# Two-step opening of the last batch sums, two bias rows moved later, and an early Gelu table load, in a four-layer transformer kernel

## Chip, cores and metric

The kernel runs on one core of one Trainium2 chip. The metric is the device time of one execution in microseconds (us); the lower, the better. Times of instructions below are from the profiled execution, counted from the start of its span.

## The reference

Eight batches of 128 tokens with 512 channels (float32) go through four layers. Each layer adds an attention and then a feed-forward to x, each of the layernorm of x. Cut to what matters here:

```python
x = x + L0_xattn(layernorm(x), ctx, ...)   # 32 heads of 128, own keys and values per head
x = x + L0_ffn(layernorm(x), ...)          # silu, 1376 hidden, low-rank parts
x = x + L1_xattn(layernorm(x), ctx, ...)   # small attention of 8 heads of 8
x = x + L1_ffn(layernorm(x), ...)          # 1792 hidden, one of each 32 picked
x = x + L2_xattn(layernorm(x), ctx, ...)   # 32 heads, 8 key heads, normed q and k
x = x + L2_ffn(layernorm(x), ...)          # mixture of low-rank experts
x = x + L3_xattn(layernorm(x), ctx, ...)   # 32 heads, 8 key heads, biases bq, bkv, bo
x = x + L3_ffn(layernorm(x), ...)          # gelu(x @ inter_w + inter_b) @ output_w + output_b
```

The row `L3_bo` is the output bias of layer 3's attention and the row `F3_bias` that of its feed-forward: each is one row of 512 numbers that is added to every token of x.

## The kernel before

x stays in SBUF, one tile of 128x512 for each batch. All products are float32 made of three passes over operands that are split into a high and a low part (fp32r): high times high, high times low, low times high. A weight tile of 128x512 is loaded by SyncE (SP) into a ring buffer and split by GpSimd (POOL), in the attentions at L698 (high part) and L700 (low part), in the feed-forwards at L1338 (low part; ScalarE (ACT) makes the high one at L1512). TensorE (PE) multiplies, ACT and VectorE (DVE) empty the PSUM banks and make high and low parts of the activations.

Each engine has one program of its own, written out by hand; within it the instructions run in the written order, and semaphores join the engines. `m.wait(engine, name, n)` lets an engine wait until n events of a name have happened.

**Attentions** (numbers 0, 2 and 3, stages 0, 4 and 6) run over 8 groups of 4 heads. A step of one head on PE is: the scores of the next head (L920), the projections that are needed next (L390), then, for each half of the batches, a transposition of the probabilities (L940, bank `turn`), which ACT copies to `ptbuf` (L1079), and the product with the values (L953, bank `heado`), whose high part ACT makes (L1081, counted as `high`) and whose low part DVE makes (L1245, counted as `low`). In its own order ACT takes both halves of the next head's exponentials (L1060) and the projected q before it copies the turned probabilities. DVE takes the maxima of the next head first (L1168, L1170), then the projected q (L1004), the low parts, and the normalisation of the next head (L1177, L1184).

After each pair of heads the pair's output sums are made: for each of the 8 batches six matmuls (two slots of `w_out` and `acts`, three passes each) go into the bank `outp[b % 2]`, DVE adds the bank to x (L1221, or L493 where sums for the next norm are taken too) and counts `added`. The sums of a pair are spread over the steps of the next pair; batch 7's stand at the end of the second step. The last pair's have no such steps: they follow in the tail (`pe_tail`, L994), all eight behind one another. Behind batches 6 and 7 and after them stand the transpositions of the next layernorm, whose deviations, Newton steps and normalisations run on ACT and DVE (L464 to L542) after batch 4 and after batch 7.

**Feed-forwards** F0 (silu, 11 chunks), F1 (pick, 14 chunks) and F3 (gelu, 16 chunks) run over chunks of 128 hidden channels: two projections of 12 matmuls (one for each half of the batches), the activation on ACT (L1534 for Gelu, into `pbuf`), its high part on ACT (L1547), its low part on DVE (L1576). A Gelu of a chunk waits until the low part of the same half of the chunk before has been made. Each pair of chunks has output sums as above (L1413, added at L1571), and the last pair's stand in the tail (L1487). F0's last pair is one chunk alone. In F3 the tail is the end of the kernel: each batch of x is stored once it has been added.

**Bias rows.** SP loads a row into `brow` for all partitions (L1664), and `add_row` (L1666 to L1670) adds it to the eight tiles of x: eight DVE instructions of 128x512, both operands in SBUF. Row 1 (`L3_bo`) is added at the start of attention 3 (L1265), ahead of DVE's copy of the first projected q. Row 2 (`F3_bias`) is added at the start of F3 (L1632), ahead of the first low parts.

**Gelu's table.** ACT has one load of a function table for the Gelu (at its first Gelu, in F3's first chunk). The norm ahead of F3 is in `act_tail` (n = 7) and uses Square, Identity and Copy.

Of the kernel before, what the change touches and what calls it, by code (L numbers as in the profile page):

```python
# [255 lines left out]
def build(nc, ins, out):  # L256

    with ExitStack() as ctx:
# [154 lines left out]

        def pe_out(pe, b, slots, last=True):

            for n, s in enumerate(slots):
                mm = pe_matmuls(pe, outp[b % 2][:, :], lambda a, c: acts[:, s, a, b * S:(b + 1) * S],
                                lambda a, c: w_out[:, s, a, :], chunks=1, first=n == 0,
                                last=last and n == len(slots) - 1)
            return mm  # L420
# [180 lines left out]
        def act_tail(act, n, wait_added):  # L601
# [19 lines left out]
            act_ln_high(act, n, 3)  # L621
            first_take(act, True, n, "k")
            for F in (F0, F1):
                if F.stage == n:
                    take_low_rank(act, F, 0)
# [230 lines left out]
        def attention_pe(pe, A):  # L856
# [136 lines left out]
            group(NG - 1)  # L993
            pe_tail(pe, A.stage + 1, lambda b: out_product(NG - 1, 1, [b]))  # L994

# [141 lines left out]
        def attention_dve(dve, A):  # L1137
# [126 lines left out]

            if A.layer == 3:  # L1265
                add_row(dve, 1)
            if A.normed:
# [18 lines left out]
            if A.normed:  # L1286
                rms(0, 1, "q")
            group(0)
            with dve.Fori(1, NG - 1) as g:
# [98 lines left out]
        def ffn_pe(pe, A):  # L1388
# [16 lines left out]

            def out_product(p, slots, bs, last):
                if bs[0] == 0:
                    m.wait(pe, "low", 4 * p + 2 * len(slots))
                    m.wait(pe, "split", A.out_tile(p, slots))
                for b in bs:  # L1410
                    m.wait(pe, "added", B * p + (b - 1))
                    more = last and A.kind == "silu"
                    mm = pe_out(pe, b, slots, last=not more)  # L1413
                    if more:
                        if b == 0:
                            m.wait(pe, "low2_low", 2)
                            m.wait(pe, "a_split", 2)
                        mm = pe.matmul(outp[b % 2][:, :], low_in[0:96, b * S:(b + 1) * S], low_b2[:, :], start=False, stop=True)
                    mm.then_inc(m["outfull"], 1)
# [142 lines left out]
        def ffn_dve(dve, A):  # L1562
# [36 lines left out]
            def chunks(g, js):  # L1599
                for j in js:  # L1600
# [28 lines left out]
                    for b in adds[BH:]:  # L1629
                        add(p, b)  # L1630

            if A.row is not None:  # L1632
                add_row(dve, A.row)
            if A.kind == "silu":
# [911 lines left out]
```

## Time and profile before

| | us |
|---|---|
| three timed runs, median (lowest to highest) | 3104.1 (3098.24 to 3104.85) |
| profiled execution, its own time | 3098.03 |
| its span | 3096.2 |
| PE busy | 2936.9 |
| DVE busy | 1727.3 |
| ACT busy | 1109.4 |
| POOL busy | 986.4 |

The times are device times of whole executions; the span is what the profile covers of one of them. An engine is busy while one of its instructions runs; PE's matmuls are pipelined and their ends modelled, so that a row of many matmuls reads somewhat longer than the time in which they are issued. The weight loads of PE (PEld) run beside the matmuls. In a row of the timeline the bracket tells how long the engine was idle before the first instruction of the row, and whose end released it.

### The profile page before, as it was taken

What the parts mean: (1) busy time and instruction counts of PE and PEld (TensorE: products, weight loads), DVE (VectorE), ACT (ScalarE), POOL (GpSimd) and SP (SyncE); (2) the same over time, 40 slices, a digit from 0 to 9 for tenths busy, and PEclk for the clock granted to TensorE, in tenths of its full rate; (3) what the DMA queues carried; (4) which work ended last, traced back from release to release, by engine and by line L of the source; (5) the groups of instructions that cost most, each with busy time, mean ns of one, the idle gap of its engine ahead of it and who ended that gap; (6) DMA issues with size and microseconds to landing.
All of it is one profiled execution on the core that took longest, in us unless ns stands there. A gap on an engine that the chain in (4) does not pass through costs nothing.

```text
span 3096.2 us, 47952 instructions
## 1 busy us (share of the span) xinstructions
PE 2936.9 (95%) x16224; PEld 2488.0 (80%) x16224; DVE 1727.3 (56%) x3514; ACT 1109.4 (36%) x3614; POOL 986.4 (32%) x836
## 2 busy tenths in 40 slices
PE   7999999999989989899889999999889999999899
PEld 6888888888878857688778888888768888888687
DVE  6544444444542278777666666666644444544644
ACT  4222222232242237622344444444423333333432
POOL 4333333333321146433233222332213333332221
PEclk9999999999999999899999999999999999999999
DMA  3111111111111101011111101110011111110111
GB/s 120 41 48 40 47 40 47 30 48 37 36 56 44 37 28 29 26 35 41 32 38 31 28 27 34 34 34 17 25 38 38 41 38 37 34 34 21 45 45 47
DMA packets 68564, 119.74 MB, mean 39 GB/s; under 512 B 8681, under 2 KB 14185, under 8 KB 68065
## 3 DMA queue, kind: packets, MB, share of 16 engines
q1 hardware_dynamic: 68450, 118.26, 12.7%
q8 instruction: 67, 1.10, 0.1%
q14 instruction: 47, 0.39, 0.0%
HBM read 116.06 MB, written 2.10 MB: 38 GB/s over the span
## 4 chain that ended last, share of the span: by engine, by line
PE 84%; DVE 8%; ACT 4%; issue 3%; DMA 0%; POOL 0%; DVEq 0%; SPq 0%; ACTq 0%; POOLq 0%
PE proj L390 38%; PE outp L390 23%; PE heado L953 6%; PE score L920 4%; PE turn L940 3%; PE score L390 2%; PE outp L1850 1%; PE score L1432 1%; PE proj L406 1%; ACT sq L1048 1%; ACT tbuf L1060 1%; PE heado L1850 1%; ACT acts L1081 1%; DVE x L1669 1%; DVE tbuf L1160 0%
## 5 line engine op out<-in xcount | busy, mean ns | idle before, releaser
L390 PE MATMUL outp<-w_out,acts 128*128 128x512 f32 x3288 | 839.7, 400 | 20.9 <-DVE x L1221 12.3
L390 PE MATMUL proj<-xnT,w_in 128*128 128x512 f32 x3192 | 760.1, 393 | 7.2 <-issue 2.3
L390 PEld LDWEIGHTS outp<-w_out,acts 128*128 128x128 f32 x3288 | 597.2, 189 | 145.1 <-DVE x L1221 14.7
L390 PEld LDWEIGHTS proj<-xnT,w_in 128*128 128x128 f32 x3192 | 594.7, 189 | 134.1 <-issue 5.3
L390 PE MATMUL proj<-ctxT,w_kv 128*128 128x512 f32 x1536 | 367.3, 395 | 25.0 <-POOL w_kv L700 18.8
L698 POOL TENSOR_TENSOR w_out<-ring,consts 128x512 fp32r<-128x512 f32 x96 | 102.1, 1064 | 837.1 <-PE outp L390 837.1
L390 PEld LDWEIGHTS proj<-ctxT,w_kv 128*128 128x128 f32 x1536 | 285.5, 189 | 89.1 <-issue 21.0
L1221 DVE TENSOR_TENSOR x<-x,outp 128x512 f32<-128x512 f32 x360 | 245.0, 686 | 186.1 <-PE outp L390 184.3
L1003 DVE COPY big<-proj 128x512 f32<-128x512 f32 x136 | 93.8, 690 | 350.2 <-PE proj L390 347.8
L698 POOL TENSOR_TENSOR w_kv<-ring,consts 128x512 fp32r<-128x512 f32 x93 | 97.2, 1045 | 461.6 <-DMA ring<-in_L_wk 441.9
L1081 ACT ACTIVATE acts<-heado 128x512 fp32r<-128x512 f32 x192 | 115.1, 599 | 324.7 <-PE heado L953 324.7
L1245 DVE TENSOR_TENSOR acts<-heado,acts 128x512 fp32r<-128x512 f32 x192 | 132.8, 692 | 174.6 <-ACT acts L1081 174.6
L953 PEld LDWEIGHTS heado<-ptbuf,big 128*128 128x128 f32 x1536 | 201.5, 192 | 30.8 <-ACT ptbuf L1079 15.9
L953 PE MATMUL heado<-ptbuf,big 128*128 128x128 f32 x1536 | 205.0, 277 | 12.6 <-ACT ptbuf L1079 7.2
L1000 ACT ACTIVATE big<-proj 128x512 f32<-128x512 f32 x136 | 80.8, 594 | 376.1 <-PE proj L390 369.4
L1079 ACT ACTIVATE ptbuf<-turn 128x512 f32<-128x512 f32 x192 | 114.4, 596 | 266.4 <-PE turn L940 266.4
L920 PEld LDWEIGHTS score<-big 128*128 128x128 f32 x1536 | 183.2, 192 | 9.0 <-issue 4.4
L920 PE MATMUL score<-big 128*128 128x128 f32 x1536 | 187.2, 275 | 3.0 <-issue 1.7
L390 PE MATMUL proj<-w_kv,ctxT 128*128 128x256 f32 x1536 | 183.4, 280 | 1.5 <-DVE big L1003 1.5
L390 PEld LDWEIGHTS proj<-w_kv,ctxT 128*128 128x128 f32 x1536 | 182.1, 188 | 3.1 <-DVE big L1003 1.9
L1571 DVE TENSOR_TENSOR x<-x,outp 128x512 f32<-128x512 f32 x160 | 109.9, 687 | 102.5 <-PE outp L390 102.1
L698 POOL TENSOR_TENSOR w_in<-ring,consts 128x512 fp32r<-128x512 f32 x96 | 106.3, 1108 | 167.4 <-PE proj L390 89.6
(294 smaller groups left out, 4125.8 us busy)
## 6 DMA issues: line engine op xcount, KB each, us to landing
ring<-in_L_wq SPq DMA_DIRECT2D x96, 256.0 KB, 2.8
ring<-in_L_wo SPq DMA_DIRECT2D x96, 256.0 KB, 2.7
ring<-in_F_in SPq DMA_DIRECT2D x52, 256.0 KB, 2.7
ring<-in_L_wk SPq DMA_DIRECT2D x48, 256.0 KB, 2.7
ring<-in_L_wv SPq DMA_DIRECT2D x48, 256.0 KB, 3.1
ring<-in_F_out SPq DMA_DIRECT2D x41, 256.0 KB, 2.6
x<-in_x SPq DMA_DIRECT2D x2, 1024.0 KB, 8.5
big<-in_ctxT SPq DMA_DIRECT2D x4, 512.0 KB, 8.2
```

Of the source, the lines that this page charges most:

```text
L390: mm = pe.matmul(bank_ap, w_ap(a, c), rhs(b, c), start=first and c == 0 and n == 0, stop=last and c == chunks - 1 and n == len(PASSES) - 1)
L698: pool.tensor_tensor(dst[:, slot, 0, :], ring[:, r, :], zeros512, ALU.add).then_inc(m["high_w"], 1)
L920: mm = pe.matmul(score[half][:, b * P:(b + 1) * P], qT[:, t], kT[:, t], start=True, stop=True)
L940: mm = pe.transpose(turn[:, b * P:(b + 1) * P], probs[j % 2][:, half, b * P:(b + 1) * P], ident)
L953: mm = pe.matmul(heado[:, b * P:(b + 1) * P], v_pair[:, n, j % 2, :] if A.own_kv else v[:, n * S:(n + 1) * S], ptbuf[:, half, b * P:(b + 1 ...
L1000: return engine.activation(dst, src, ACT.Copy)
L1003: return engine.tensor_copy(dst, src)
L1079: act.activation(ptbuf[:, half, :], turn[:, :], ACT.Copy).then_inc(m["tfree"], 1)
L1081: act.activation(acts[:, j, 0, half * HALF:(half + 1) * HALF], heado[:, :], ACT.Copy)\
L1221: dve.tensor_tensor(x[:, b, :], x[:, b, :], outp[b % 2][:, :], ALU.add).then_inc(m["added"], 1)
L1245: dve.tensor_tensor(acts[:, j, 1, cols], heado[:, :], acts[:, j, 0, cols].bitcast(F32), ALU.subtract)\
L1571: dve.tensor_tensor(x[:, b, :], x[:, b, :], outp[b % 2][:, :], ALU.add).then_inc(m["added"], 1)
```

## The change

- `pe_out` gets a parameter `first`, so that a bank can be opened by one call and finished by another.
- In the tails of the three attentions (`last_product`) and of F1 and F3 (`opened` in `out_product`), batches 0 and 1 get the three matmuls of the pair's first slot, in both banks, before PE waits for the low parts of the second slot. Then the three matmuls of the second slot follow for batch 0 and batch 1. Batches 2 to 7 are as before. Batch 0 is opened once batch 6 of the pair before has been added, batch 1 once batch 7 has.
- `add_row` of row 1 moves behind the normalisations of head 0 of attention 3, ahead of the first group of steps.
- `add_row` of row 2 moves behind the two low parts of F3's first chunk.
- ACT gets one Gelu of a single column (into `rq`, which isn't used there), in the norm ahead of F3, behind the high parts of batches 0 to 3 and ahead of the normalisations of batches 5 and 7.

```diff
--- before.py
+++ after.py
@@ -411,11 +411,11 @@
                                stop=last and c == DC - 1)
             return mm
 
-        def pe_out(pe, b, slots, last=True):
+        def pe_out(pe, b, slots, last=True, first=True):
 
             for n, s in enumerate(slots):
                 mm = pe_matmuls(pe, outp[b % 2][:, :], lambda a, c: acts[:, s, a, b * S:(b + 1) * S],
-                                lambda a, c: w_out[:, s, a, :], chunks=1, first=n == 0,
+                                lambda a, c: w_out[:, s, a, :], chunks=1, first=first and n == 0,
                                 last=last and n == len(slots) - 1)
             return mm
 
@@ -620,6 +620,8 @@
             deviations(7)
             act_ln_high(act, n, 3)
             first_take(act, True, n, "k")
+            if F3.stage == n:
+                act.activation(rq[:, 0:1], consts[:, C_ONES:C_ONES + 1], ACT.Gelu_apprx_tanh)
             for F in (F0, F1):
                 if F.stage == n:
                     take_low_rank(act, F, 0)
@@ -991,7 +993,22 @@
             with pe.Fori(1, NG - 1) as g:
                 group(g)
             group(NG - 1)
-            pe_tail(pe, A.stage + 1, lambda b: out_product(NG - 1, 1, [b]))
+            def last_product(b):
+
+                p = 2 * (NG - 1) + 1
+                if b == 0:
+                    m.wait(pe, "low", 4 * p + 2)
+                    m.wait(pe, "split", A.tile(NG - 1, 3, "o") + 1)
+                    for k in range(2):
+                        m.wait(pe, "added", B * p + (k - 1))
+                        pe_out(pe, k, (2,), last=False)
+                    m.wait(pe, "low", 4 * (p + 1))
+                if b < 2:
+                    pe_out(pe, b, (3,), first=False).then_inc(m["outfull"], 1)
+                    return
+                out_product(NG - 1, 1, [b])
+
+            pe_tail(pe, A.stage + 1, last_product)
 
         def copy_projection(engine, on_act, dst, src, bias):
 
@@ -1262,8 +1279,6 @@
                 for j in range(GH):
                     step(g, j)
 
-            if A.layer == 3:
-                add_row(dve, 1)
             if A.normed:
                 dve.wait_ge(ln_low, 8 * ln_no(A.stage) + B)
                 rms(0, 0, "k")
@@ -1285,6 +1300,8 @@
                 normalise(0, 0, half)
             if A.normed:
                 rms(0, 1, "q")
+            if A.layer == 3:
+                add_row(dve, 1)
             group(0)
             with dve.Fori(1, NG - 1) as g:
                 group(g)
@@ -1404,13 +1421,23 @@
                     mm.then_inc(m["lowfull"], 1)
 
             def out_product(p, slots, bs, last):
+                opened = last and len(slots) == 2
                 if bs[0] == 0:
+                    if opened:
+                        m.wait(pe, "low", 4 * p + 2)
+                        m.wait(pe, "split", A.out_tile(p, slots))
+                        for b in range(2):
+                            m.wait(pe, "added", B * p + (b - 1))
+                            pe_out(pe, b, slots[:1], last=False)
                     m.wait(pe, "low", 4 * p + 2 * len(slots))
                     m.wait(pe, "split", A.out_tile(p, slots))
                 for b in bs:
                     m.wait(pe, "added", B * p + (b - 1))
                     more = last and A.kind == "silu"
-                    mm = pe_out(pe, b, slots, last=not more)
+                    if opened and b < 2:
+                        mm = pe_out(pe, b, slots[1:], first=False)
+                    else:
+                        mm = pe_out(pe, b, slots, last=not more)
                     if more:
                         if b == 0:
                             m.wait(pe, "low2_low", 2)
@@ -1628,9 +1655,9 @@
                         low_part(c, j, half)
                     for b in adds[BH:]:
                         add(p, b)
-
-            if A.row is not None:
-                add_row(dve, A.row)
+                    if A.row is not None and first:
+                        add_row(dve, A.row)
+
             if A.kind == "silu":
                 for half in range(2):
                     take_low_part(dve, A, half)
```

## Rows read from the trace of the kernel before

**Rows 1.** The page: busy time by engine; engines' shares of the last chain.
```profile
PE 2936.9 (95%) x16224; PEld 2488.0 (80%) x16224; DVE 1727.3 (56%) x3514; ACT 1109.4 (36%) x3614; POOL 986.4 (32%) x836
...
PE 84%; DVE 8%; ACT 4%; issue 3%; DMA 0%; POOL 0%; DVEq 0%; SPq 0%; ACTq 0%; POOLq 0%
```

**Rows 2.** Timeline, end of attention 0: start, length, instruction, count [idle before <-releaser].
```profile
874.74 9.40 PEld L390 LDWEIGHTS outp<-w_out,acts 128*128 128x128 f32 x42 [0.46 <-DVE acts L1245]
...
874.82 0.69 DVE L1221 TENSOR_TENSOR x<-x,outp 128x512 f32<-128x512 f32 x1
...
876.51 0.69 DVE L493 SCALAR_TENSOR_TENSOR x<-outp,x 128x512 f32<-128x512 f32 x1 [1.01 <-PE outp L390]
...
877.89 0.69 DVE L493 SCALAR_TENSOR_TENSOR x<-outp,x 128x512 f32<-128x512 f32 x1 [0.68 <-PE outp L390]
```

**Rows 3.** Timeline, end of F1.
```profile
1514.31 8.00 PE L390 MATMUL outp<-w_out,acts 128*128 128x512 f32 x28 [4.53 <-DVE acts L1576]
1517.35 0.69 DVE L493 SCALAR_TENSOR_TENSOR x<-outp,x 128x512 f32<-128x512 f32 x1 [3.09 <-PE outp L390]
...
1518.83 0.69 DVE L493 SCALAR_TENSOR_TENSOR x<-outp,x 128x512 f32<-128x512 f32 x1 [0.78 <-PE outp L390]
```

**Rows 4.** Windows, behind F1's idle time: busy by engine, granted clock, DMA.
```profile
1513.90:1517.40 3.50, 3.09 (x8) 2.48 (x9) 0.41 (x2) 0.00 (x0) 0.00 (x0) 0.51 0.24 80
```

**Rows 5.** Timeline, end of F3.
```profile
3081.78 11.22 PE L390 MATMUL outp<-w_out,acts 128*128 128x512 f32 x48 [2.62 <-DVE acts L1576]
3083.56 0.69 DVE L1571 TENSOR_TENSOR x<-x,outp 128x512 f32<-128x512 f32 x1 [1.83 <-PE outp L390]
```

**Rows 6.** Timeline, start of attention 3.
```profile
2312.68 4.90 DVE L1669 TENSOR_TENSOR x<-x,brow 128x512 f32<-128x512 f32 x8
...
2316.47 2.02 POOL L698 TENSOR_TENSOR w_in<-ring,consts 128x512 fp32r<-128x512 f32 x1 [38.58 <-PE proj L410]
...
2317.62 0.75 DVE L1004 TENSOR_SCALAR big<-proj,vecs 128x512 f32<-128x512 f32 x1
...
2318.52 2.02 PE L920 MATMUL score<-big 128*128 128x128 f32 x16 [0.35 <-DVE big L1004]
```

**Rows 7.** Timeline, attention 3 behind its first normalisations.
```profile
2328.78 1.48 POOL L698 TENSOR_TENSOR w_out<-ring,consts 128x512 fp32r<-128x512 f32 x1
...
2330.32 0.37 ACT L1060 ACTIVATE pbuf<-score,negmax 128x128 f32<-128x128 f32 x1 [4.90 <-DVE negmax L1170]
...
2332.71 1.29 POOL L700 TENSOR_TENSOR w_kv<-ring,w_kv 128x512 fp32r<-128x512 f32 x1
...
2334.24 0.60 PE L940 MATMUL turn<-consts,tbuf 128*128 128x128 f32 x4
...
2334.88 0.60 ACT L1079 ACTIVATE ptbuf<-turn 128x512 f32<-128x512 f32 x1 [1.07 <-PE turn L940]
```

**Rows 8.** Timeline, start of F3.
```profile
2909.08 0.81 ACT L514 ACTIVATE tbuf<-x,recentre,rstd 128x512 f32<-128x512 f32 x1 [3.21 <-DVE recentre L473]
...
2913.72 1.30 POOL L1338 TENSOR_TENSOR w_out<-ring,w_out 128x512 fp32r<-128x512 f32 x1 [24.36 <-ACT w_out L1512]
2914.10 8.98 DVE L1669 TENSOR_TENSOR x<-x,brow 128x512 f32<-128x512 f32 x8
2914.19 1.28 ACT L1534 ACT_TABLE_LOAD   x1
...
2914.98 1.73 POOL L1338 TENSOR_TENSOR w_in<-ring,w_in 128x512 fp32r<-128x512 f32 x1
...
2916.76 5.74 PE L390 MATMUL proj<-xnT,w_in 128*128 128x512 f32 x24 [0.52 <-POOL w_in L1338]
...
2917.39 1.14 ACT L1547 ACTIVATE acts<-pbuf 128x512 fp32r<-128x512 f32 x2
...
2923.11 1.29 DVE L1576 TENSOR_TENSOR acts<-pbuf,acts 128x512 fp32r<-128x512 f32 x2
...
2924.73 5.69 PE L390 MATMUL proj<-xnT,w_in 128*128 128x512 f32 x24 [2.23 <-ACT pbuf L1534]
```

## Prediction

> **What bounds the kernel now.** I read the page first. The first part shows TensorE (PE) busy 95% of the span, and the chain that ended last lies 84% on PE and 8% on VectorE (DVE) [rows 1]. So an edit counts only where PE waits, or where it makes PE wait. I then read the timeline at each place that the diff touches: the end of an attention, the ends of the feed-forwards F1 and F3, and the first steps of attention 3 and of F3. At each place the reader should look for two things: the idle time in brackets behind a PE row, and which instruction of another engine ends just before it. All sums are made against the profiled execution (3098.03 us, span 3096.2). The median of the three timed runs is 3104.1 and their lowest is 3098.24, so the profiled one is at their fast edge.
>
> **Opened sums at the end of the three attentions.** The edit saves time only if PE idles before the last pair. Here it doesn't: batch 7 of the pair before runs just ahead, and PE idles for at most 0.46 us of weight loading behind the last DVE low part [rows 2]. The matmuls themselves run nearly through. What the edit adds are two dependences.
> - Batch 1 can be opened only in the bank that batch 7 of the pair before still holds. DVE adds that batch at 874.82 for 0.69, until 875.51 [rows 2]. Before the change a whole batch (six matmuls) covered this add. A batch costs 1.38, the distance of two adds [rows 2], so three matmuls cost 0.69. Now only these three cover it.
> - Batch 2 needs bank 0, so batch 0's add. That starts 876.51 - 874.74 - 1.38 = 0.39 after a batch's last matmul is issued and takes 0.69 [rows 2]. A whole batch covered it; now the three matmuls that finish batch 1 do.
>
> Step by step for attention 0: batch 7 ends about 874.43, batch 0 is opened until 875.12, PE waits until 875.57 (the add plus 0.06), opens batch 1 until 876.26, finishes batch 0 at 876.95 and batch 1 at 877.64; batch 0 is added at 877.34 to 878.03, and batch 2 starts about 878.1. Before, it started at 874.74 + 2 x 1.38 = 877.5. That is 0.6 later. The norm behind it waits for batch 4, so nothing takes the delay back. The other two attentions have the same order (one pattern, three places): **+1.9** in all. Bounds: 0 if a wait ends earlier than I think, +2.7 if both waits cost fully.
>
> **Opened sums at the end of F1.** PE idles 4.53 us for DVE's low parts, and the batch sums then start at half clock: the granted clock is 0.51, so the level of 1.2 GHz, from 1513.9 to 1517.4 [rows 3, 4]. The banks are free early, so six matmuls (1.38 at full clock) go into the idle time. Before, batch 0 was added at 1517.35 and batch 1 at 1518.83, so batch 2 started about 1518.83 - 0.39 = 1518.4 [rows 3]. If the clock still falls, three half-clock matmuls (1.3) finish batch 0 at 1515.6, batch 1 at 1516.9, and batch 2 starts there with 0.2 left to run slowly: **-1.3**. If the opened matmuls keep the clock at 2.4 GHz, batch 2 starts near 1516.2: -2.1. I take -1.3, since 3.2 us of idle time are still left.
>
> **Opened sums at the end of F3.** PE idles 2.62 us [rows 5]; six matmuls go in. Batch 0 ends at 3081.78 + 0.69 = 3082.47, its add runs from 3082.87 to 3083.56, and batch 2 starts at 3083.6 instead of 3081.78 + 2.76 = 3084.54: **-0.9**. Without that new wait it would be -1.38.
>
> **Bias row in attention 3.** Eight adds of 128x512 take 4.90 us in the old place [rows 6]. There they hold back DVE's copy of q (2317.62) and so PE's scores (2318.52, 0.35 idle before). By the issue of the turns before them, 0.2 ahead of their modelled end, the idle time is some 0.5, so moving the adds gives **-0.5**. In the new place they stand in DVE's queue behind the two first normalisations and ahead of the maxima of head 1. Queued behind the row are DVE's maxima, then ScalarE's (ACT) exponentials of head 1, and behind those, in ACT's own order, the copy of the turned head 0, which PE's heado matmul waits for [rows 7]. Now ACT starts the exponentials at 2330.32, is done about 2333.8, and waits 1.07 for PE at 2334.88 [rows 7]. So the slack is 1.07. The DVE queue moves by 4.90, less 0.1 for overlap. The slack takes 1.07: about **+3.9** of PE idle time (2334.3 to 2338.9 in the shifted clock, 4.6 in all). A comparable idle time, 4.53, was followed by half clock [rows 3, 4]; PE has some 2.7 us of work in such a stretch, so I add half of that, **+1.3** (bounds 0 and +2.7). No PE work can come forward, since its order is fixed.
>
> The unknown is GpSimd (POOL). From 2328.78 to 2334.00 it splits weights there, four instructions almost without a pause [rows 7], and both engines' operands lie in SBUF. In the old place of F3's row, four POOL instructions of L1338 stretch the same eight adds to 8.98 [rows 8]. But in the old place of attention 3 an L698 waits (2.02 long) and the adds keep their 4.90 [rows 6]. The first POOL instruction at the new place is an L698 [rows 7], so I take 4.90. If POOL gets through between every two adds, each add waits for one, 1.04 to 1.30 long: 8 x 1.1 = 8.8 more. So this edit is -0.5 + 3.9 + 1.3 = **+4.7**, between +2.5 and +13.5.
>
> The Trainium skill (SBUF — State Buffer, "SBUF: two separate sides") says that VectorE with two SBUF inputs and GpSimd lock one shared port pair, that whichever starts first holds it for its instruction, and that the other blocks fully. The stretched adds agree with that. It doesn't say who wins between two queued adds; that choice is the rival below.
>
> **Bias row in F3.** In the old place it takes 8.98 us [rows 8]; it stretches POOL's split of w_in to 1.73 (1.30 alone), for which PE waits 0.52, and delays the low parts to 2923.11, for which PE waits 2.23 behind the Gelu [rows 8]. Both waits go: chunk 1 starts about 2916.3, chunk 2 at 2921.8 instead of 2924.73. Then the row itself is late. The low parts of chunk 0 end at about 2921.2 (two POOL instructions in between), the adds take 4.90 plus two POOL instructions of 1.3, until 2928.6, and the low parts of chunk 1 (0.69 each) end about 2929.9. The first output sum needs them: it starts at 2929.9 instead of about 2930.3. **-0.5**. If POOL doesn't interfere at all, it starts at the end of chunk 2's matmuls or up to 2 us earlier: -2.
>
> **Gelu table.** The load takes 1.28 us and ends at 2915.47, before the first Gelu [rows 8]. But the second Gelu waits for PE's second half, which ends at about 2916.2 (2916.76 less the 0.52 of idle time), so ACT's next work starts as before: 0. In the new place it falls into ACT's idle time of 3.21 before 2909.08 [rows 8], also 0; without that cover it would cost 1.5. A reload for the norms would cost another 1.28, which I don't expect, since Copy runs behind the Gelu without one [rows 8].
>
> **Sum.** +1.9 - 1.3 - 0.9 + 4.7 - 0.5 + 0 = **+3.9 us**. Against the profiled execution that is 3101.9; against the median, 3104.1 + 3.9 = **3108.0**.
>
> **Rivals.**
> - Alternation: POOL gets the port between all adds of attention 3's row. Then the sum is 3.9 + 8.8 = +12.7: 3116.8. For it: four L1338 stretch the adds in F3 [rows 8]. Against it: the L698 at 2316.47 didn't [rows 6]. It decides when POOL gets through more than two or three times.
> - Hidden row: ACT and DVE find the time in attention 3 (the delayed exponentials lie beside PE's projection after all), so that edit is -0.5, and the attention tails cost nothing. Then -0.5 - 1.3 - 0.9 - 0.5 = -3.2: 3100.9. With F1's clock kept up and the F3 row at -2 it is -5.5, and with the tails gaining their 0.69 each -7.6: 3096.5. For it: PE has a projection of 24 matmuls (5.5 us at 0.23 each) just then; against it: ACT's order.
> - Slower through the tails: the two bank waits cost fully in all attentions and the clock falls for a double stretch in attention 3 (half rate for all its work): +2.7 - 1.3 - 0.9 + 6.1 - 0.5 = +6.1: 3110.2, from which on it counts as slower.
>
> **How the numbers follow.** A measurement of this kernel can tell about 0.2% (6.2 us) from no change. Forecast 0.50, alternation 0.22, hidden 0.18 (a third of it beyond -6.2), slower tails 0.10. The first is within 0.2%, with some of it above; so faster 0.09, same 0.61, slower 0.30. The range 3098.5 to 3117.5 leaves out the far end of the hidden case and takes in the alternation.
>
> **What would show it.** In the timeline of the changed kernel: a PE wait between batch 7's and batch 0's matmuls in the attention tails, ended by a DVE add of x; six output matmuls inside the idle time of F1's and F3's ends; in attention 3 the row behind the first L1184 pair with 4.9 to 13 us, and PE waiting for ACT's ptbuf copy some 4 us and more; in F3 no wait at chunk 2 but one before the first output sums. The prediction is wrong if PE doesn't wait in attention 3's first step, or if the row there is stretched to twice its time.

## Result and profile after

The changed kernel is slower. Its median is 3113.6 us (3110.2 to 3120.4) beside 3098.4 (3097.6 to 3104.9) of the kernel before in the same series: a ratio of 1.0048, 95% interval 1.0038 to 1.0058, so 14.9 us (11.8 to 18.0). The profiled execution took 3118.38 us, its span 3116.5.

The first step is to ask where the time lies. Both kernels run the same 16224 matmuls in the same order but for a few at the tails, so the start of each matmul can be subtracted from that of the same one before. The steps of this difference, against the profiled execution of before (the step of a wait is read at the first matmul behind it, and what the next ones lose further is put down to half clock):

| place | forecast | measured |
|---|---|---|
| tail of attention 0 | +0.6 | +0.6, taken back by the norm: 0.0 |
| end of F1 | -1.3 | -2.2, and -0.9 later |
| tail of attention 2 | +0.6 | +0.4 |
| mixture (F2) | 0 | +9.8 |
| start of attention 3 | -0.5 | -0.6 |
| attention 3, PE's wait in the first step | +3.9 | +11.3 |
| half clock behind it | +1.3 | +2.6 |
| tail of attention 3 | +0.6 | +0.6 |
| start of F3 with its bias row | -0.5 | -0.7 |
| half clock behind F3's first outputs | 0 | +1.7 |
| tail of F3 | -0.9 | -0.9 |

The steps add up to +21.1. With -0.6 that lies ahead of attention 0, and small differences between the places, that is the +20.4 between the two profiled executions. The medians lie 15 apart. The mixture's +9.8 is a matter of the execution, as is shown below.

First the page of the changed kernel, busy time by engine and the engines' shares of the last chain, as in [rows 1]:

```profile
PE 2952.2 (95%) x16224; PEld 2501.0 (80%) x16224; DVE 1730.7 (56%) x3514; ACT 1109.1 (36%) x3615; POOL 987.9 (32%) x836
...
PE 83%; DVE 9%; ACT 4%; issue 3%; POOL 0%; DMA 0%; DVEq 0%; SPq 0%; ACTq 0%; POOLq 0%
```

PE has the same 16224 matmuls and is busy 15.3 us longer, which is mostly half clock. The other 5 us are idle time of PE, net. DVE's share of the chain grows from 8 to 9%. Lines of the changed kernel stand 2 to 27 further down: L1669 of before is L1696, L1079 is L1096, L953 is L955.

**Attention 3**, in the timeline of the changed kernel. The columns are start, length, engine, line, operation, count, and in brackets the idle time before and who ended it. These rows answer [rows 6, 7]:

```profile
2324.36 1.95 PE L922 MATMUL score<-big 128*128 128x128 f32 x16
...
2335.06 12.58 DVE L1696 TENSOR_TENSOR x<-x,brow 128x512 f32<-128x512 f32 x8
2336.11 1.63 POOL L702 TENSOR_TENSOR w_out<-ring,w_out 128x512 fp32r<-128x512 f32 x1
2337.70 1.49 POOL L700 TENSOR_TENSOR w_kv<-ring,consts 128x512 fp32r<-128x512 f32 x1
...
2339.26 1.60 POOL L702 TENSOR_TENSOR w_kv<-ring,w_kv 128x512 fp32r<-128x512 f32 x1
...
2348.61 0.37 ACT L1077 ACTIVATE pbuf<-score,negmax 128x128 f32<-128x128 f32 x1 [17.41 <-DVE negmax L1187]
...
2352.63 2.08 PE L955 MATMUL heado<-ptbuf,big 128*128 128x128 f32 x8 [12.02 <-ACT ptbuf L1096]
```

The scores no longer wait. The eight adds take 12.58 instead of 4.90, and beside them POOL's splits run one behind the other at a distance of 1.57 (2336.11, 2337.70, 2339.26). Twelve and a half divided by eight is 1.57 too: one add and one POOL instruction take turns. Behind the row stand the maxima, then ACT's exponentials (idle for 17.41), then ACT's copy of the turned head, and PE waits 12.02 for that copy. From the trace of the kernel before, the two rows that stand right ahead of the new place, and PE's wait for the same copy:

```profile
2327.21 1.59 POOL L700 TENSOR_TENSOR w_in<-ring,w_in 128x512 fp32r<-128x512 f32 x1
2327.80 1.55 DVE L1184 TENSOR_TENSOR tbuf<-tbuf,rinv 128x512 f32<-128x512 f32 x1
...
2335.53 1.16 PE L953 MATMUL heado<-ptbuf,big 128*128 128x128 f32 x8 [0.69 <-ACT ptbuf L1079]
```

PE waited 0.69 at this matmul before, so the change adds 11.3. The other two rows show engines that take turns already: the normalisation L1184 took 1.55 behind the L700 (the one of the other half, at 2326.92, took 0.76), and the L698 behind it took 1.48 [rows 7], where an L698 alone takes 1.04.

**The tails.** The first group is attention 0 [rows 2], the second the end of F1 [rows 3], the third the end of F3 [rows 5], all from the timeline of the changed kernel:

```profile
874.88 2.35 PE L390 MATMUL outp<-w_out,acts 128*128 128x512 f32 x9 [0.15 <-DVE x L1238]
...
877.40 6.87 PE L390 MATMUL outp<-w_out,acts 128*128 128x512 f32 x29 [0.17 <-DVE x L493]
...
882.65 0.17 DVE L468 TENSOR_SCALAR nw_v<-sqdev 128x4 f32<-128x4 f32 x1
...
1510.40 2.14 DVE L1603 TENSOR_TENSOR acts<-pbuf,acts 128x512 fp32r<-128x512 f32 x2
1510.43 1.56 POOL L700 TENSOR_TENSOR w_in<-ring,consts 128x512 fp32r<-128x512 f32 x1
...
1513.84 0.69 DVE L493 SCALAR_TENSOR_TENSOR x<-outp,x 128x512 f32<-128x512 f32 x1 [1.30 <-PE outp L390]
...
3103.01 1.65 PE L390 MATMUL outp<-w_out,acts 128*128 128x512 f32 x6 [1.27 <-DVE acts L1603]
...
3104.83 1.42 PE L390 MATMUL outp<-w_out,acts 128*128 128x512 f32 x5 [0.16 <-DVE x L1598]
```

In attention 0 PE now waits twice for an add of DVE, where it ran through before: the two dependences of the forecast. In F3 the wait for the low parts shrank from 2.62 to 1.27 (six matmuls went in), and batch 2 waits for an add. At the end of F1 one thing is new. DVE's two low parts took 3.25 before and take 2.14 now. The same rows of before:

```profile
1511.00 1.04 POOL L698 TENSOR_TENSOR w_in<-ring,consts 128x512 fp32r<-128x512 f32 x1
1511.00 3.25 DVE L1576 TENSOR_TENSOR acts<-pbuf,acts 128x512 fp32r<-128x512 f32 x2
...
883.27 0.17 DVE L468 TENSOR_SCALAR nw_v<-sqdev 128x4 f32<-128x4 f32 x1 [0.60 <-ACT ptbuf L499]
```

Before, POOL and DVE started together and POOL ran at once (1.04), so DVE stood behind it first and again behind the next split. Now DVE is 0.03 earlier and gets its first low part through. This alone is 1.1 of the 2.2 us. The last line is attention 0's norm before the change: DVE waited 0.60 there for ACT's deviations. In the changed kernel, at 882.65, it doesn't, which is where attention 0's delay went.

**F3's start**, timeline of the changed kernel, and a window (us, busy by engine, granted clock, DMA share, GB/s), beside [rows 8]:

```profile
2926.18 1.28 ACT L624 ACT_TABLE_LOAD   x1
...
2936.62 11.17 PE L390 MATMUL proj<-xnT,w_in 128*128 128x512 f32 x48
...
2941.34 7.09 DVE L1696 TENSOR_TENSOR x<-x,brow 128x512 f32<-128x512 f32 x8
...
2949.81 6.44 PE L390 MATMUL outp<-w_out,acts 128*128 128x512 f32 x20 [2.02 <-DVE acts L1603]
...
2950.00:2954.00 4.00, 4.00 (x11) 3.15 (x11) 0.69 (x1) 2.61 (x5) 2.57 (x2) 0.57 0.07 19
```

Chunks 1 and 2 are one row of 48 matmuls without a wait; the wait stands before the first outputs, as forecast. Behind it the granted clock is 0.57, mostly the level of 1.2 GHz.

**The mixture** isn't touched by the diff. Before, then after; each as the transpositions of its norm, the 96 small matmuls behind them, and a window of 12 us:

```profile
2237.55 1.11 PE L527 MATMUL turn<-consts,tbuf 128*128 128x128 f32 x4 [4.85 <-DVE tbuf L506]
...
2240.88 10.94 PE L390 MATMUL proj<-w_in,xnT 128*128 128x136 f32 x96
...
2242.00:2254.00 12.00, 12.00 (x99) 11.59 (x99) 4.65 (x12) 0.00 (x0) 0.00 (x0) 1.00 0.00 1
```

```profile
2234.32 1.11 PE L527 MATMUL turn<-consts,tbuf 128*128 128x128 f32 x4 [4.84 <-DVE tbuf L506]
...
2237.65 20.73 PE L390 MATMUL proj<-w_in,xnT 128*128 128x136 f32 x96
...
2242.00:2254.00 12.00, 12.00 (x58) 12.00 (x57) 1.50 (x5) 0.00 (x0) 0.00 (x0) 0.50 0.00 0
```

Both idle 4.85 us (4.84 after) before the transpositions and both transpose at half clock (1.11 for four). Before, the clock is back at 2.4 GHz for the 96 matmuls: 10.94. After, PE runs all 96 without a pause at 1.2 GHz: 20.73.

### The profile page after: what moved, and what is told of

Its sections match the earlier page's. It is cut to its first block, busy times and chain, and to the rows that moved or that the text cites. A ratio compares the mean times of both kernels' runs of the same rounds, so it can differ in the third digit from the quotient of the medians.

```text
span 3116.5 us, 47955 instructions
## 1 busy us (share of the span) xinstructions
PE 2952.2 (95%) x16224; PEld 2501.0 (80%) x16224; DVE 1730.7 (56%) x3514; ACT 1109.1 (36%) x3615; POOL 987.9 (32%) x836
## 3 DMA queue, kind: packets, MB, share of 16 engines
q1 hardware_dynamic: 68450, 118.26, 12.7%
## 4 chain that ended last, share of the span: by engine, by line
PE 83%; DVE 9%; ACT 4%; issue 3%; POOL 0%; DMA 0%; DVEq 0%; SPq 0%; ACTq 0%; POOLq 0%
PE proj L390 37%; PE outp L390 23%; PE heado L955 6%; PE score L922 4%; PE turn L942 2%; PE score L390 2%; PE proj L406 1%; PE outp L1877 1%; PE score L1459 1%; DVE x L1696 1%; ACT sq L1065 1%; ACT tbuf L1077 1%; PE heado L1877 1%; ACT acts L1098 1%; ACT xnT L535 0%
## 5 line engine op out<-in xcount | busy, mean ns | idle before, releaser
L700 POOL TENSOR_TENSOR w_out<-ring,consts 128x512 fp32r<-128x512 f32 x96 | 102.5, 1068 | 838.4 <-PE outp L390 838.4
L390 PEld LDWEIGHTS proj<-ctxT,w_kv 128*128 128x128 f32 x1536 | 285.5, 189 | 88.5 <-issue 20.4
L700 POOL TENSOR_TENSOR w_kv<-ring,consts 128x512 fp32r<-128x512 f32 x93 | 97.6, 1049 | 470.5 <-DMA ring<-in_L_wk 450.4
L955 PEld LDWEIGHTS heado<-ptbuf,big 128*128 128x128 f32 x1536 | 201.9, 193 | 42.1 <-ACT ptbuf L1096 27.2
L955 PE MATMUL heado<-ptbuf,big 128*128 128x128 f32 x1536 | 205.5, 277 | 23.9 <-ACT ptbuf L1096 18.5
L1096 ACT ACTIVATE ptbuf<-turn 128x512 f32<-128x512 f32 x192 | 114.4, 596 | 266.1 <-PE turn L942 266.1
L700 POOL TENSOR_TENSOR w_in<-ring,consts 128x512 fp32r<-128x512 f32 x96 | 106.3, 1108 | 175.2 <-PE proj L390 100.4
```

The costliest lines, as they stand in the source:

```text
L390: mm = pe.matmul(bank_ap, w_ap(a, c), rhs(b, c), start=first and c == 0 and n == 0, stop=last and c == chunks - 1 and n == len(PASSES) - 1)
L700: pool.tensor_tensor(dst[:, slot, 0, :], ring[:, r, :], zeros512, ALU.add).then_inc(m["high_w"], 1)
L955: mm = pe.matmul(heado[:, b * P:(b + 1) * P], v_pair[:, n, j % 2, :] if A.own_kv else v[:, n * S:(n + 1) * S], ptbuf[:, half, b * P:(b + 1 ...
L1096: act.activation(ptbuf[:, half, :], turn[:, :], ACT.Copy).then_inc(m["tfree"], 1)
```

## Experiments

All but the ninth were timed over several rounds beside the kernel before; where shifts are given they are of the same matmuls, as in the table above. The medians of the kernel before move between the series (3098.4 to 3103.0), so only ratios are compared.

**1. The row move of attention 3 alone.**

```diff
@@ attention, DVE's program
-            if A.layer == 3:
-                add_row(dve, 1)
...
                 rms(0, 1, "q")
+            if A.layer == 3:
+                add_row(dve, 1)
             group(0)
```

> The kernel before with one edit: attention 3's bias row behind the first normalisations. Theory (port): POOL gets between all of the eight adds, so they take 12 to 13 us instead of 4.90, PE waits about 12 us for the turned probabilities in the first step, and some half-clock time behind it costs 1 to 3 more: 12 to 15 us slower than before, most of what the whole change costs. Rival (queue alone): the adds keep 4.90 and the edit costs 4.7. Rival (clock chance): the edit costs 5 or less and the rest of the whole change's 15 us comes from the mixture stage, where its profile showed a long half-clock stretch.

Measured, over four executions: 3114.9 us beside 3101.3, ratio 1.0049 (1.0032 to 1.0066). From its timeline:

```profile
2330.97 12.59 DVE L1669 TENSOR_TENSOR x<-x,brow 128x512 f32<-128x512 f32 x8
...
2348.54 2.07 PE L953 MATMUL heado<-ptbuf,big 128*128 128x128 f32 x8 [12.02 <-ACT ptbuf L1079]
```

The shifts are -0.6, +11.3 and +2.8 (half clock). The row move alone is as slow as the whole change, with the same 12.59 and 12.02.

**2. The same move, without the shared port.** The adds of row 1 take a PSUM bank in place of the row in SBUF. The bias row of layer 3's attention is left out and old sums are added instead; the instructions, their sizes and their places are the same.

```diff
-                dve.tensor_tensor(x[:, b, :], x[:, b, :], brow[:, :], ALU.add).then_inc(row_added, 1)
+                dve.tensor_tensor(x[:, b, :], x[:, b, :], outp[b % 2][:, :] if n == 1 else brow[:, :], ALU.add).then_inc(row_added, 1)
```

> As e1, but the eight adds at the new place read their second operand from a PSUM bank (the sums left in outp) instead of brow in SBUF, so that the bias row of attention 3 is left out and replaced by old sums; the place in the queue and the number of instructions stay. Theory (port): without a second SBUF operand POOL can't hold them up: 4.9 to 5.5 us for the eight, PE idle 4 to 5 us in the first step, 3.4 slower than before, up to 6 where the clock falls behind it. Rival (the place in the queue alone costs it all): still 12 to 15 us slower.

Measured: ratio 1.0023 (1.0013 to 1.0032). Its timeline:

```profile
2329.70 4.86 DVE L1669 TENSOR_TENSOR x<-x,outp 128x512 f32<-128x512 f32 x8
2330.75 1.29 POOL L700 TENSOR_TENSOR w_out<-ring,w_out 128x512 fp32r<-128x512 f32 x1
...
2334.90 1.04 POOL L698 TENSOR_TENSOR w_in<-ring,consts 128x512 fp32r<-128x512 f32 x1 [0.48 <-PE proj L390]
...
2340.02 2.08 PE L953 MATMUL heado<-ptbuf,big 128*128 128x128 f32 x8 [4.76 <-ACT ptbuf L1079]
```

With one operand outside SBUF the adds take 4.86 and POOL's splits their own 1.29 and 1.04, side by side. PE's wait is 4.76, and its shifts are -0.6, +4.1 and +2.9 of half clock. This splits the loss: the place in DVE's queue costs 4.1 (4.76 less the 0.69 of before), and taking turns with POOL 7.3 more (12.02 less 4.76). The Trainium skill (SBUF — State Buffer, "SBUF: two separate sides") says that a DVE operation locks the pair of ports against a GpSimd operation when it has two inputs in SBUF. The pair of experiments 1 and 2 agrees with that: 12.59 against 4.86.

**3. The changed kernel without that move.** Row 1 is back at its old place, all else is as after.

```diff
--- after
+            if A.layer == 3:
+                add_row(dve, 1)
             if A.normed:
...
-            if A.layer == 3:
-                add_row(dve, 1)
             group(0)
```

> The changed kernel with attention 3's bias row back in its old place; all else of the change kept. Theory: F1's tail -2.2 and up to -0.9 more of clock, F3's tail -0.9, F3's row -0.5 to +1, attention tails +0.4 and +0.6 where they count: 1 to 4 us faster than before. Rival (the tails shift the mixture stage into a long half-clock stretch, as the changed kernel's profile showed once): 6 to 8 us slower than before in the median.

Measured: ratio 1.0006 (0.9994 to 1.0017), no change that can be measured, where 1 to 4 us faster was expected. The ten executions fall into two groups: six from 3096.2 to 3101.0 and four from 3106.8 to 3109.0. The profiled one is of the first and holds no long stretch at half clock in the mixture. A distance of 8 us is about what the long stretch costs (+9.8); for the second group it is inferred, since no such execution of this kernel was profiled.

**4. The opened sums alone**, in all five places, with both rows and the table as before.

```diff
-        def pe_out(pe, b, slots, last=True):
+        def pe_out(pe, b, slots, last=True, first=True):
...
-            pe_tail(pe, A.stage + 1, lambda b: out_product(NG - 1, 1, [b]))
+            pe_tail(pe, A.stage + 1, last_product)
...
+                opened = last and len(slots) == 2
```

> The kernel before with the opened sums alone (three attentions, F1, F3); rows and table as before. Theory: attention 0 is absorbed (ACT's deviations are late there), attention 2 +0.4, attention 3 +0.6, F1 -2.2, F3 -0.9: about 2 us faster than before. PE waits for added batches 7 and 0 (0.15 and 0.2 idle) show in each attention tail. Rival (these edits bring the long half-clock stretch of the mixture): 5 to 8 us slower.

Measured: ratio 0.9998 (0.9988 to 1.0008), where 2 us faster was expected and isn't excluded, with executions from 3097.0 to 3106.3. The profiled one has the long stretch again, and by the window it is the same one:

```profile
2239.96 20.73 PE L390 MATMUL proj<-w_in,xnT 128*128 128x136 f32 x96
...
2242.00:2254.00 12.00, 12.00 (x58) 12.00 (x58) 1.50 (x5) 0.00 (x0) 0.00 (x0) 0.50 0.00 0
```

So it isn't a matter of attention 3's row, which lies behind it. In this execution the other tails gave less than 0.1 (attention 0), -2.2 (F1), +0.4 and +0.6 (attentions 2 and 3) and -0.9 (F3), and the mixture +9.8.

**5. The opened sums of attention 2 alone**, the tail just ahead of the mixture.

```diff
-            pe_tail(pe, A.stage + 1, lambda b: out_product(NG - 1, 1, [b]))
+            pe_tail(pe, A.stage + 1, last_product if A.layer == 2 else lambda b: out_product(NG - 1, 1, [b]))
```

> The kernel before with the opened sums in attention 2's tail alone. Theory (the 0.4 to 0.6 us by which this tail shifts the mixture's first transpositions decides whether its 96 small matmuls run at half clock): most executions +0.4, but three to five in ten some 10 us longer, which none of the runs of before was. Rival (F1's earlier end brings it): no execution above 3105.

Measured: ratio 1.0009 (1.0000 to 1.0019). The tail's own cost is +0.62 - 0.26 = +0.4. One execution of ten took 3110.1, the others 3099.1 to 3104.4. That is fewer than expected: these openings alone don't bring the long stretch often.

**6. The opened sums of F1 and F3 alone.**

```diff
-        def pe_out(pe, b, slots, last=True):
+        def pe_out(pe, b, slots, last=True, first=True):
...
+                opened = last and len(slots) == 2
```

> The kernel before with the opened sums in F1 and F3 alone. Theory: -2.2 and -0.9, about 3 us faster than before in nearly all executions, no long half-clock stretch in the mixture. Rival (F1's earlier end brings that stretch): a third of the executions 7 us slower.

Measured: ratio 0.9989 (0.9980 to 0.9998), -3.4 us, and executions from 3093.2 to 3098.9 without a second group. In its profiled execution F3's tail gives -0.9, but F1's -1.5 (at the start of batch 2) is followed by +1.5 of half clock. There the two low parts took 3.26. In the other five profiles with an opened F1 they took 2.14, in all seven without it 3.22 to 3.25; POOL's split starts 0.04 or less from DVE's in each of them, and the low parts took 2.14 wherever DVE's started first. The gain at F1 thus has a part of 1.1 us that a tie of a few hundredths decides.

**7. Row 1 in two halves**: four adds at the old place, four behind the first maxima.

```diff
             if A.layer == 3:
-                add_row(dve, 1)
+                add_row(dve, 1, range(4))
...
             for half in range(2):
                 scores(0, 0, half)
+            if A.layer == 3:
+                add_row(dve, 1, range(4, B))
```

> The kernel before with attention 3's row in two parts: four adds in the old place, four behind the first maxima of head 0 and ahead of the second q. Theory: all eight keep 0.61 each, since POOL is idle there, PE's scores no longer wait for the row: -0.5 to -0.6, same within what can be measured, and PE doesn't wait in the first step. Rival (any later place lets POOL in): the second four take 6 us and PE waits 2 and more.

Measured: ratio 0.9998 (0.9988 to 1.0007). The timeline shows both halves at their own length, and scores without a wait:

```profile
2312.89 2.49 DVE L1671 TENSOR_TENSOR x<-x,brow 128x512 f32<-128x512 f32 x4
...
2318.21 1.95 PE L920 MATMUL score<-big 128*128 128x128 f32 x16
...
2321.36 2.48 DVE L1671 TENSOR_TENSOR x<-x,brow 128x512 f32<-128x512 f32 x4
```

The 0.6 us at the start is had without the wait. By itself that is too little to be measured.

**8. F3's row alone.**

```diff
                     for b in adds[BH:]:
                         add(p, b)
+                    if A.row is not None and first:
+                        add_row(dve, A.row)
-            if A.row is not None:
-                add_row(dve, A.row)
```

> Only F3's bias row is moved behind the first chunk's weights; nothing else is changed. The theory expects the first chunk about 0.5 us earlier, the matmuls of the second chunk to run straight on, the row's adds at about 7 us instead of 9, the first outputs to wait about 2 us for them or for the activations, and up to 1.5 us at half clock behind that wait: between -0.5 and +1.0 us, ratio within 0.0005 of 1. The rival of the prediction for this step, that the adds meet GpSimd's steps as in attention 3, expects the adds at 12 us and the sum at +5 or more.

Measured: ratio 1.0010 (1.0001 to 1.0020), so +3 us with an interval that reaches down to +0.3. The timeline, and the window behind the wait:

```profile
2915.77 11.17 PE L390 MATMUL proj<-xnT,w_in 128*128 128x512 f32 x48
...
2920.48 7.09 DVE L1669 TENSOR_TENSOR x<-x,brow 128x512 f32<-128x512 f32 x8
...
2928.96 12.96 PE L390 MATMUL outp<-w_out,acts 128*128 128x512 f32 x48 [2.02 <-DVE acts L1576]
...
2929.00:2933.00 4.00, 4.00 (x11) 3.12 (x12) 0.69 (x1) 2.76 (x6) 2.45 (x2) 0.62 0.06 19
```

The shifts are -0.44 (chunk 1), -0.30 (first outputs) and +1.75 (half clock): in this execution the half clock behind the wait costs more than the move gives back, +1.0 in all. The adds meet two POOL instructions that stand apart, and take 7.09, not 12. The +3 lies above the -0.5 to +1.0 that was expected. This execution is 2.1 longer than the profiled one of before, and +1.6 of that is a second stretch at half clock, behind the unchanged wait of 2.62 in F3's tail (granted clock 0.57 from 3083 to 3087), where no other profile loses time. Experiment 10 bears on the row too.

**9. The Gelu table alone.** Of this kernel there is one execution.

```diff
+            if F3.stage == n:
+                act.activation(rq[:, 0:1], consts[:, C_ONES:C_ONES + 1], ACT.Gelu_apprx_tanh)
```

> Only the Gelu table is asked for ahead of the last norms; nothing else is changed. The prediction gave it 0: expected is the table's load in ScalarE's idle time before norm 5's work, and the same times of the matmuls of F3 to within 0.1 us. The rival, that the load was on the path at F3's start, expects F3's first chunk up to 1.3 us earlier; one that the earlier load stands ahead of the norms' work expects it up to 1.3 us later.

```profile
2907.49 1.28 ACT L624 ACT_TABLE_LOAD   x1
2908.78 0.20 ACT L624 ACTIVATE rq<-consts 128x1 f32<-128x1 f32 x1
2910.69 0.81 ACT L514 ACTIVATE tbuf<-x,recentre,rstd 128x512 f32<-128x512 f32 x1 [1.70 <-DVE recentre L473]
```

The load and its Gelu take 1.5 of ACT's idle time and leave 1.70. F3's matmuls start at the same time to 0.02 (shift 1.61 ahead of F3, 1.59 to 1.60 at its chunks 1 and 2 and its first outputs). It brings nothing and costs nothing.

**10. The feed-forward part of the change**, with the early table: after, without the row move of attention 3 and without the openings in the attentions.

```diff
--- after
-            pe_tail(pe, A.stage + 1, last_product)
+            pe_tail(pe, A.stage + 1, lambda b: out_product(NG - 1, 1, [b]))
...
+            if A.layer == 3:
+                add_row(dve, 1)
             if A.normed:
```

> The changed kernel with two of its parts taken out: attention 3's bias row is back ahead of the scores, and the last pair's sums in the attentions are as before. What is left is the opened sums of F1 and F3, F3's bias row behind the first chunk, and the early Gelu table. The theory (attention tails cost about 0.4 to 0.6 us each, F1's opened sum returns 2 to 3, F3's 0.9, F3's row returns 0.5 at its start and is followed by up to 1.5 at half clock behind the wait of the first outputs) expects 2 to 3 us under the kernel before, near 3097, with no execution that holds the long stretch at half clock in the mixture. The rival, that F3's row costs more than its start returns, expects this kernel 1 us or more above the one with the opened sums of F1 and F3 alone (ratio 0.9989), so at 1.000 or above.

Measured: ratio 0.9983 (0.9974 to 0.9993), -5.3 us. All ten executions lie between 3094.4 and 3099.7. The rival expected 1.000 or above. The kernel lies 0.0006 below that of experiment 6, which has neither F3's row move nor the table, with an uncertainty of 0.0013; so the +3 of experiment 8 isn't confirmed here, and whether the row's move in F3 costs anything in the median stays open. The difference to experiment 3, which holds the attentions' openings besides, is 0.0023, some 7 us with an uncertainty of about 5. Their own delays in the profiles (0.0, +0.4, +0.6) are 1 us of that. The rest fits the long stretch in some of its executions, which isn't shown.

**11. What the runs recommend**: the opened sums in F1 and F3 only, row 1 in two halves as in experiment 7, F3's row spread as two adds behind the low parts of each of the first four chunks, and the early table.

```diff
+                    if A.row is not None and isinstance(c, int) and c < 4:
+                        add_row(dve, A.row, range(2 * c, 2 * c + 2))
-            if A.row is not None:
-                add_row(dve, A.row)
```

> Made from what the runs showed: sums opened in F1 and F3 alone; four adds of attention 3's row in the old place and four behind the first maxima, where DVE and POOL are both idle for some 3.8 us; two adds of F3's row behind the low parts of each of the first four chunks; the early Gelu table. Theory: F1 -2.2 (with clock up to -3), F3's tail -0.9, attention 3 -0.6, F3's start -2 to -3 (neither the chunk 2 wait nor the one before the first output sums): 5.5 to 7 us faster than before, ratio 0.998. Rival (the mixture's long half-clock stretch comes with any shift ahead of it): a third of the executions are 10 us longer and the median gains nothing.

Measured: 3092.4 us beside 3099.6, ratio 0.9977 (0.9968 to 0.9986): 7 us faster than before and some 22 faster than after. Its timeline at F3's start:

```profile
2916.14 1.28 DVE L1683 TENSOR_TENSOR x<-x,brow 128x512 f32<-128x512 f32 x2
...
2921.97 1.28 DVE L1683 TENSOR_TENSOR x<-x,brow 128x512 f32<-128x512 f32 x2
2922.45 11.20 PE L390 MATMUL outp<-w_out,acts 128*128 128x512 f32 x48
```

Each pair of adds falls where POOL is idle (1.28 for two) and nothing behind it is waited for. PE starts the first outputs without a wait, at full clock. The shift at F3's start is -3.5, where the moved row gave -0.7 and then +1.7.

## Why the prediction was right or wrong

The kernel came out slower, inside the range of 3098.5 to 3117.5 but 5.6 above the forecast of 3108.0. The working is weaker than that sounds. The forecast added +3.9 to a median of 3104.1, and the same kernel had a median of 3098.4 beside the changed one. The true difference was +14.9, nearest to the alternation rival's +12.7. That 3108.0 comes so near is luck: the base was 5.7 too high, and of the difference the forecast had a quarter. The likeliest case was the wrong one, and by the prediction's own sign, "if the row there is stretched to twice its time", it failed: the row took 12.58, 2.6 times its 4.90.

- **The step that failed** is "The first POOL instruction at the new place is an L698 [rows 7], so I take 4.90". It drew a rule about a kind of instruction from a single L698 that waited [rows 6]. That one arrived alone, during the seventh of the eight adds, and waited for the eighth too. At the new place POOL runs eight splits one behind the other beside the adds, and both L698 and L700 take turns with the adds. The rival priced this at 8 x 1.1 = 8.8; measured are 12.58 - 4.90 = 7.7 on the row and 12.02 - 4.76 = 7.3 on PE's wait. The rows that should have decided were those of F3's old place, where the adds meet four splits [rows 8], the cited L698 itself, which is 1.48 long because it took turns with a normalisation (shown with attention 3 above), and above all the count of the splits that stand at the new place.
- **The queue delay** was right: 4.6 of idle time and +3.9 of shift forecast, 4.76 and +4.1 in experiment 2. DVE's row holds the maxima, these ACT's exponentials, and these the copy that PE waits for, with the slack of 1.07 worked out.
- **Half clock behind that wait**: 1.3 forecast, 2.6 to 2.9 measured in three kernels, so twice the term and at its upper bound of 2.7 or just above. A wait of 12 is followed by no more loss (2.6, 2.8) than one of 4.8 (2.9). The lower bound of +2.5 for this edit has no working: the terms give -0.5 + 3.9 + 0 = 3.4.
- **Attention tails**: 0.6 each was right at batch 2 in all three. The sentence "the norm behind it waits for batch 4, so nothing takes the delay back" was wrong for attention 0, where DVE waited 0.60 for ACT's deviations anyway, and for attention 2, where 0.25 came back. The sum is +1.0, not +1.9.
- **F1**: -1.3 forecast, -2.2 measured (the case of a kept clock, given as -2.1, is 1516.2 - 1518.4 = -2.2 by its own numbers). The half clock still came, as forecast (0.50 from 1513.2 to 1516.6, beside [rows 4]). The excess is one POOL instruction of 1.1 that DVE's low parts no longer stood behind. The prediction named the low parts as the end of the wait and didn't read what stretched them. The further -0.9 is a short stretch at half clock near 1578 of before (granted clock 0.81 from 1577 to 1586) that the changed kernel doesn't have (1.00 from 1574 to 1583). It isn't shown to come from the opened sums: the profiles of experiments 1, 7 and 9, with F1 as before, don't have it at that place either, and stand at half clock for longer behind F1's wait instead (in experiment 1 from 1513 to 1519).
- **F3's tail**: -0.9 forecast, -0.9 measured in the changed kernel and in experiments 3, 4, 6, 10 and 11.
- **F3's row**: -0.5 forecast, -0.7 measured at the first outputs (-0.4 of it at chunk 1). The forecast's own times, 2929.9 and 2930.3, give -0.4. The adds took 7.09 (4.90 + 2 x 1.3 = 7.5 was the working). What was missing is the +1.7 at half clock behind a wait of 2.02. A stretch like it had been priced in attention 3 and not here, because the old wait at the same spot of the pipeline (2.23, [rows 8]) wasn't followed by one. That was so in this execution only: in the profile of experiment 7 the same wait, 2.22, is followed by half clock (granted clock 0.59 from 2924 to 2928, +1.6). Of the profiles with the row moved whole all four have it behind the first outputs, of the eight with the row in its old place one has it, behind chunk 2's wait.
- **The table**: 0, as forecast.
- **The mixture**, +9.8 in the profiled execution: not foreseen at all. Half clock was looked for behind each wait that changes, not in a stage that the diff leaves alone.

What is shown and what isn't: that the row move is the loss, and how it splits into queue and port, is shown by experiments 1 and 2. That the mixture's long stretch costs 10 us is shown by two profiles. What sets it off is open. Among the thirteen profiles it is in two, both with all the attention tails opened; experiment 5 has one execution of ten that may be it. Experiments 8 and 1, without any opened tail, have executions up to 3108.6 and 3120.6 whose reason no profile shows, so the link to the attention tails is not proven. The profiles show another thing that goes with it: when the clock fell in PE's idle time before the transpositions. In the two with the long stretch it fell 0.5 us after PE's last matmul (at 2230.0 in the changed kernel, at 2232.3 in experiment 4), in the eleven others 0.8 to 1.8 us after it (1.4 before the change, at 2234.1). An edit anywhere ahead might move the work against the clock's fall, and so might chance. This is a coincidence of thirteen profiles, and no run tests it.

## What to carry to other kernels

Before an elementwise step with two SBUF operands is moved, count the GpSimd instructions that stand ready at its new place: each can cost the step one of their lengths, once for every instruction of its own. Cut such a row into pieces and put each where GpSimd is idle and where the instruction behind it has slack; two at a time with GpSimd idle cost 0.64 each here, eight in a bunch beside eight GpSimd instructions 1.57 each. And in these runs a sum that is opened early paid only where TensorE waited for the second part for longer than the banks took to come free.

## What the runs showed of the hardware

- DVE and POOL took turns, one instruction each, on queued work with SBUF operands: 1.57 us for each pair of an add (0.61 alone) and a split (1.04 or 1.29 alone), in eight pairs. Turns aren't shown for every arrival: the single split that came during the seventh of eight adds waited for the eighth too (2.02 long, [rows 6]).
- An instruction of one of them that starts 0.03 us before the other's decides 1.1 us (F1's low parts, 2.14 or 3.25).
- TensorE at 1.2 GHz stayed there through 96 matmuls of 128x136 that it ran without a pause for 20.73 us, after 4.84 us of idle time, while the same work in the kernel before went back to 2.4 GHz at its start. The Trainium skill (TensorE: Matmul & The Clock Gate, "Part 1: The HAM clock gate") gives the recent activity of TensorE as what sets its clock. The busy time of the profile doesn't tell that activity here: a window that reads 12.00 of 12.00 busy was granted 0.50 in one kernel and 1.00 in the other. What went with the long stretch is when the clock had fallen: 0.5 us after the last matmul before the idle time in two profiles, 0.8 to 1.8 in eleven.
- Waits of 2.0 us of TensorE were followed by half clock in some places (0.57 and 0.62 behind F3's first outputs in two kernels) and a wait of 2.23 in the kernel before [rows 8] by none (granted clock 1.00 from 2926 to 2931). The same wait in experiment 7, 2.22 long, was followed by half clock (0.59 from 2924 to 2928). The length of a wait alone doesn't tell.
